# Router logits with the gate as the stationary operand in four column groups, small transfers in front of large ones, and the loop bodies reordered

## The reference, cut to what matters

```python
x = x + xattn(layernorm(x), ctx)      # Q, K, V projections, FFT over the sequence,
                                      # two Hamilton products, a filter, inverse FFT
x = x + ffn(layernorm(x))             # a router and 8 experts
# in ffn:
tokens = layer_norm(inputs.reshape(-1, 512), gamma, beta)
logits = tokens @ gate_weight.T                     # [16384, 8], float32
top1 = argmax(logits);  weight = softmax(logits)[top1]
rank = running count of tokens per expert;  keep = rank < 1024
dispatch[top1, rank] = tokens                       # 8 experts x 1024 slots
h = gelu(dispatch @ wi) ;  expert_out = h @ wo      # 512 -> 2048 -> 512
out = inputs + weight * expert_out[top1, rank]
```

## Time and profile before

| | us |
|---|---|
| median of 3 runs | 3565.24 (3561.56 to 3566.55) |
| profiled execution, its own time | 3560.93 |
| span of the profiled execution | 3559.1 |
| PE busy | 3459.5 (97%) |
| DVE busy | 2547.8 (72%) |
| ACT busy | 1610.9 (45%) |
| POOL busy | 1264.8 (36%) |

### The profile page before, as it was taken

The page is one execution under the profiler, slowest core; times in us unless marked ns, Lnnn a source line. Parts: engine busy times, 40 slices in busy tenths (PEclk is TensorE's granted clock), DMA queues, the critical chain, the costliest instruction groups (busy, mean ns, idle before and its releaser), DMA issues. The chain is left out here.

```text
span 3559.1 us, 46918 instructions
## 1 busy us (share of the span) xinstructions
PE 3459.5 (97%) x15056; PEld 2634.4 (74%) x15056; DVE 2547.8 (72%) x3536; ACT 1610.9 (45%) x2948; POOL 1264.8 (36%) x1607
## 2 busy tenths in 40 slices
PE   7999999999999999999999959999999999999998
PEld 5766777767776777776777648888888888888886
DVE  4999999999999999989899954444444444444443
ACT  4545545455454554545545333333333333333332
POOL 2556656466565565656566530000000000000000
PEclk9999999999999999999999969999999999999999
DMA  5421221211212112121121123333333333333331
GB/s 201 153 104 59 73 83 59 81 62 59 83 48 95 60 59 95 71 83 48 59 95 60 60 81 104 109 119 118 120 119 119 117 119 106 107 105 119 107 108 41
DMA packets 223433, 326.65 MB, mean 92 GB/s; under 512 B 36880, under 2 KB 102672, under 8 KB 223280
## 3 DMA queue, kind: packets, MB, share of 16 engines
q1 hardware_dynamic: 207952, 307.97, 25.1%
q0 software_dynamic: 15360, 16.99, 1.4%
HBM read 256.82 MB, written 101.97 MB: 101 GB/s over the span
## 5 line engine op out<-in xcount | busy, mean ns | idle before, releaser
L1372 ACT ACTIVATE act<-hid_ps 128x512 f32<-128x512 f32 x256 | 153.1, 598 | 797.5 <-PE hid_ps L1299 797.5
L1433 DVE CAST act_h<-act 128x512 fp32r<-128x512 f32 x256 | 109.3, 427 | 523.2 <-ACT act L1372 523.2
L1253 POOL TENSOR_TENSOR tally<-tally,unit 1x1 f32<-1x1 f32 x16 | 2.9, 180 | 1350.2 <-DVE mixed L1445 1350.2
L468 PE MATMUL pair<-w_q,q_spec 128*128 128x512 f32 x1024 | 457.6, 595 | 11.6 <-DVE s L989 10.7
L1299 PE MATMUL hid_ps<-tok_h,w_h 128*128 128x512 f32 x1024 | 405.5, 396 | 0.2 <-issue 0.2
L1299 PE MATMUL hid_ps<-tok_l,w_h 128*128 128x512 f32 x1024 | 399.3, 390 | 0.0
L1299 PE MATMUL hid_ps<-tok_h,w_l 128*128 128x512 f32 x1024 | 398.7, 389 | 0.0
L1315 PE MATMUL out_ps<-w_l,act_h 128*128 128x512 f32 x1024 | 398.5, 389 | 0.0
L1314 PE MATMUL out_ps<-w_h,act_l 128*128 128x512 f32 x1024 | 398.3, 389 | 0.0
L1313 PE MATMUL out_ps<-w_h,act_h 128*128 128x512 f32 x1024 | 398.3, 389 | 0.0
L1427 DVE TENSOR_TENSOR w_l<-w_raw,w_h 128x2048 fp32r<-128x2048 f32 x128 | 293.4, 2293 | 90.9 <-ACT w_h L1366 90.9
(11 more groups left out here) (172 smaller groups left out, 7931.5 us busy)
## 6 DMA issues: line engine op xcount, KB each, us to landing
w_raw<-in_L_ffn_wi SPq DMA_DIRECT2D x128, 512.0 KB, 3.5
w_raw<-in_L_ffn_wo SPq DMA_DIRECT2D x128, 512.0 KB, 4.5
w_raw<-in_x SPq DMA_DIRECT2D x32, 1024.0 KB, 5.4
w_raw<-in_ctx SPq DMA_DIRECT2D x32, 1024.0 KB, 7.7
x_res<-in_x SPq DMA_DIRECT2D x31, 1024.0 KB, 9.8
out<-x_res SPq DMA_DIRECT2D x31, 1024.0 KB, 4.3
slots<-rows SPq DMA_DIRECT2D x4, 4160.0 KB, 17.3
got<-slots SPq DMA_DIRECT2D x15, 1040.0 KB, 7.6
```

Of the source, the lines that this page charges most:

```text
L468: last = nc.tensor.matmul(pair[k % 2][:, s, :], spec[:, c, tile * 256 + s * P:tile * 256 + (s + 1) * P], w[:, c, :], start=(c == 0 and n = ...
L1253: nc.gpsimd.tensor_tensor(tally[:], tally[:], unit[:], ALU.add).then_inc(tallied, 1)
L1372: nc.scalar.activation(act32[i % 2][:], hid_ps[i % 2][:], ACT.Gelu).then_inc(gelu, 1)
L1433: v.tensor_copy(act_h[i % 4][:], act32[i % 2][:]).then_inc(ah_ready, 1)
```

## The change

1. **Logits.** The gate is now the stationary operand, padded with zeros from 8 to 32 columns (`gate_w`), and 256 tokens are streamed at once. The four blocks of 128 features go to four column groups of the array (`tile_position=(0, 32 * c)`) and end as four partial sums on partitions 32c to 32c+31 of `even_ps`, 4 matmuls for each half sequence. When both halves are there, ACT copies `even_ps` to SBUF (`logits_out`, into the first half of `x_tok_t`, called `parts`), and PE adds the four partial sums and turns the result in one product (`logits_turn`): `parts` stationary, 128 x 128, with the 0/1 matrix `chosen` of 8 columns streamed, four of them, into columns 64 to 95 of `odd_ps`. `choose` reads the logits there. The two new semaphores are `logit_ev` and `logit_ready`; one small constant more is loaded.
2. **SP's list.** `real_store` and `real_out` come first, `real_spread` stands before `load_x`, and `real_spread`, `real_gather` belong to sequence b-2 instead of b-3; `load_c` stands before `load_x`.
3. **Bodies.** The bodies of PE, ACT, POOL and DVE are written in a new order, given in full below. On PE the order of a sequence is spread over bodies b to b+4, with `project(k=4)` split over two bodies, and the turns and logits no longer stand together. `choose(b - 3)` stands at the end of DVE's body, `scatter(b - 5)` replaces `scatter(b - 3)` on POOL.

```diff
+            gate_w = sb("gate_w", [P, CB, 32])
+            gate_g = gate_w[:, :, 0:EXPERTS]
+            chosen = sb("chosen", [P, EXPERTS])
...
-            x_tok_t = [sb(f"x_tok_t{i}", [P, CB, P]) for i in (0, 1)]
+            x_tok_t = sb("x_tok_t", [P, 2, CB, P])
+            parts = x_tok_t[:, 0].rearrange("p c e -> p (c e)")
...
                     def body(b):    # SP
-                        real_spread(b - 3)
-                        real_gather(b - 3)
                         real_store(b - 3)
+                        real_out(b - 2)
                         store(b - 4)
-                        real_out(b - 2)
+                        load_c(b)
+                        real_spread(b - 2)
                         load_x(b)
-                        load_c(b)
                         load_res(b - 3)
+                        real_gather(b - 2)
...
                     # inverse(b, 0, 0) now waits for the copy of the logits
-                                pe.wait_ge(route, (b - 1) * ROUTE + 1)
+                                pe.wait_ge(logit_ev, b)
...
-                    def logits(b, t):
-                        pe.wait_ge(g_ev, b * 4 + t + 1)
-                        if t == 0:
+                    def logits(b, h):
+                        pe.wait_ge(g_ev, b * 4 + 2 * h + 2)
+                        if h == 0:
                             pe.wait_ge(unfold, b * UNF + UNF)
                         for c in range(CB):
-                            last = nc.tensor.matmul(even_ps[:, t * EXPERTS:(t + 1) * EXPERTS], x_tok_t[t % 2][:, c, :],
-                                                    gate_g[:, c, :], start=(c == 0), stop=(c == CB - 1))
+                            last = nc.tensor.matmul(even_ps[32 * c:32 * c + 32, h * 256:h * 256 + 256], gate_w[:, c, :],
+                                                    x_tok_t[:, :, c, :], start=True, stop=True, tile_position=(0, 32 * c))
                         last.then_inc(logit_mm, 1)
+                    def logits_turn(b):
+                        pe.wait_ge(logit_ev, b + 1)
+                        for t in range(ROWT):
+                            o = LOGITS + t * EXPERTS
+                            last = nc.tensor.matmul(odd_ps[:, o:o + EXPERTS], parts[:, t * P:(t + 1) * P], chosen[:],
+                                                    start=True, stop=True)
+                        last.then_inc(logit_ready, 1)
...
                     # ACT
                     def token_block(b, t):
                         act.wait_ge(g_mm, b * 4 + t + 1)
-                        wait(act, logit_mm, b * 4 + t - 1)
+                        if t < 2:
+                            wait(act, logit_ready, b)
+                        else:
+                            act.wait_ge(logit_mm, b * 2 + 1)
...
+                    def logits_out(b):
+                        act.wait_ge(logit_mm, b * 2 + 2)
+                        nc.scalar.activation(parts, even_ps[:], ACT.Copy).then_inc(logit_ev, 1)
```

More of the change, by code:

```diff
@@ L544, in body @@
                     def body(b, p):
-                        logits(b - 3, 1)
-                        logits(b - 3, 2)
+                        project(b - 2, 4, 1)
+                        dft(b - 1, 1, 0)
+                        dft(b - 1, 1, 1)
+                        ranks(b - 4)
+                        project(b - 2, 5, 0)
+                        project(b - 2, 5, 1)
+                        inverse(b - 3, 0, 1)
+                        dft(b - 1, 1, 2)
+                        dft(b - 1, 1, 3)
@@ new lines, in body @@
+                        inverse(b - 3, 1, 0)
+                        inverse(b - 3, 1, 1)
+                        turn(b - 3, 1 - p, 0)
+                        project(b - 1, 0, 0)
+                        project(b - 1, 0, 1)
+                        turn(b - 3, 1 - p, 1)
+                        turn(b - 3, 1 - p, 2)
+                        project(b - 1, 1, 0)
+                        project(b - 1, 1, 1)
+                        logits(b - 3, 0)
+                        project(b - 1, 2, 0)
@@ L557, in body @@
+                        inverse(b - 2, 0, 0)
+                        project(b - 1, 3, 1)
+                        project(b - 1, 4, 0)
                         dft(b, 0, 3)
[L558 to L577, removed]
@@ L578, in _ @@
-                    for b in range(6):
+                    for b in range(7):
                         body(b, b % 2)
[L580 to L583, removed]
+                    with pe.Fori(7, 29, 2) as b:
+                        body(b, 1)
+                        body(b + 1, 0)
+                    for b in range(29, BATCH + 4):
                         body(b, b % 2)
@@ L728, in body @@
[L728 to L734, removed]
                         spectrum(b - 1, 1, 0)
                         spectrum(b - 1, 1, 1)
+                        real_part(b - 2, 4)
+                        context_high(b - 1)
                         spectrum(b - 1, 1, 2)
-                        real_part(b - 2, 4)
+                        real_part(b - 2, 5)
@@ L739, in body @@
                         spectrum(b - 1, 1, 3)
+                        sums_x(b)
+                        squares_x(b)
                         token_block(b - 3, 0)
                         sums_x2(b - 3, 1 - p)
[L742 to L745, removed]
                         token_block(b - 3, 1)
                         real_part(b - 1, 0)
-                    for b in range(7):
+                        real_bin(b - 1, 0)
@@ L749, in _ @@
+                        base_of(b - 3, 1 - p)
+                        q_of(b)
+                        real_part(b - 1, 3)
+                        exps(b - 3)
+                        spectrum(b, 0, 2)
+                        spectrum(b, 0, 3)
+                    for b in range(6):
                         body(b, b % 2)
[L750 to L753, removed]
+                    with act.Fori(6, 30, 2) as b:
+                        body(b, 0)
+                        body(b + 1, 1)
@@ L754, in _ @@
+                    for b in range(30, BATCH + 3):
                         body(b, b % 2)
@@ L894, in body @@
                     def body(b, p):
-                        mean2(b - 3)
-                        mean1(b)
[L897 to L903, removed]
+                        stats1(b - 1)
+                        mean2(b - 4)
+                        start1(b - 1)
+                        stats2(b - 4, p)
+                        scales1(b - 1)
+                        scatter(b - 5, 1 - p)
+                        real_bins(b - 2)
+                        mean1(b)
+                    for b in range(8):
                         body(b, b % 2)
-                    with pool.Fori(6, 30, 2) as b:
+                    with pool.Fori(8, 30, 2) as b:
                         body(b, 0)
                         body(b + 1, 1)
-                    for b in range(30, BATCH + 3):
+                    for b in range(30, BATCH + 5):
                         body(b, b % 2)
```

84 lines of the change are left out of this document (45 added, 39 removed).

## The result

The changed kernel takes 3477.58 us (median of 4 runs, 3476.09 to 3477.75) against 3563.4 for the kernel before beside it: a ratio of 0.9759, 95% interval 0.9742 to 0.9776, 86 us faster. The forecast was 3541, range 3498 to 3580. The direction was right, the size was off by more than a factor of three.

What follows compares the result with a forecast made beforehand. PE was taken to bound the first part. Logits -13, array changes +21, waits -15, clock -9, start -3, end -5 gave -24 from 3560.9: 3537, or 3541 on the median's scale; range 3498 to 3580 us.

Steps and rivals of the forecast that it cites:

- Logits on PE: PE's logits calls and logits_turn: 2.97 us a sequence, 0.41 less than before, -13 us in all.
- five steps of 0.216, 1.08 us: One logits call on PE: second pass of each group runs beside the next group's first, no wider.
- rival 1: Logits on PE: all four column groups run at once, -55 us in place of -13, time 3499; chance 0.18.
- My bound for it by weight loads: Logits on PE: loads every 0.1 us, 0.8 us a group, would hold the -55 at about -30, time 3524.
- Rival 2: Logits on PE: the four groups run one after the other, +28 us in place of -13, time 3582; chance 0.16.
- its limit for "slower": Serial logits case: slower from 0.7 us a body more than before, drains included; its own case was 1.54 us.
- Going in and out: PE array: four layout changes a body at 0.16 us each, +21 us (0 to +45).
- Waits and the new order: PE's 17.7 us of waits fall to about 3 with choose at DVE's end: -15 us (-18 to +15).
- The margins I worked out for DVE: DVE's results ready before PE needs them, every margin about 2 us or more.
- The clock: PE's five falls to half clock in the steady part vanish, 1.8 us each: -9 us (-9 to 0).
- SP's order: SP's transfer list: real-bin transfers come one body earlier, load_res directly follows load_x, nobody waits: 0 us.
- Start and end: Start: PE's 3.96 us wait for w_vl, -3 us (-5 to 0); end of first part: -5 us (-12 to +6).

Runs made afterwards that it cites:

- runs 5 and 6: Changed kernel with two column groups instead of four, two feature blocks in each, issued 0,0,1,1 and 0,1,0,1: 3501.72 and 3501.85 us.
- run 1: Changed kernel's new order with the old logits product (turned tokens stationary, 8 gate columns streamed), no logits_turn: 3543.09 us, 0.9932 of the kernel before.
- run 9: Changed kernel with SP's old list: 3475.23 us, 0.9722 of the kernel before.
- runs 1 and 10: Run 10, beside run 1: changed kernel with four transposes for logits_turn and one more DVE reduction adding the partial sums: 3474.29 us.

## Why the prediction was wrong

**Logits on PE: the step that failed.** I put a call at five steps of 0.216, 1.08 us, because "PE starts matmuls in order" and the two passes of a matmul share a group. The second half is true, the first is not: runs 5 and 6 show that each column group works through its own sequence whatever the order of issue. A call takes 0.57. The term was to be -13; the product's calls come to 2 x 0.57 + 0.81 = 1.95 against 3.40, -46 us over 32 sequences. This was rival 1's mechanism, to which I gave 0.18. My bound for it by weight loads was wrong too: a load for one group of 32 columns does take 0.11 us, but the loads of the four groups run beside each other as well, and all eight lie within 0.16 us. (Rival 2 has a slip: the other terms give 1.0 us a body, so its limit for "slower" is 1.0 and not 0.7; its price and time don't use it.)

The Trainium skill's page "TensorE: Matmul & The Clock Gate", section on packing small matmuls, has four row tiles of 512 columns 3.07 times and three column tiles 2.38 times as fast as one after the other. The traces here agree in kind: four column groups take 0.57 us and one takes 1.85, 3.2 times as much. The same section of the Trainium skill says that matmuls start and end strictly in program order; runs 5 and 6 differ from that, for groups of columns at least, and the measurement decides.

**Going in and out.** I took 0.16 us for each change, +21 us. A call takes 0.14 more than its two passes of 0.216, the `dft` in front of it 0.09 more than usual, and the one behind it 0.02 more than behind the old product: 0.25 a call, 16 us in 64 calls, of which 9 stand within the 0.57 already. With a slow start of 0.09 behind `logits_turn`, 3 us, this makes the product worth 46 less some 10 us; run 1 has 1.11 us a body, 35.5. Right in kind, and near in size.

**Waits and the new order: a term that was sized too small.** I forecast -15, with 3 us of waits left. PE waits for nothing, and run 1 has a body 1.1 us shorter than before (62.10 against 63.2 without falls), 31 us over 28 bodies, although has 17.7 in all. The error is in how I read the earlier trace rows. They count the time in which PE has no record under way, and a record runs on after the next one could have started. What a wait costs is seen from one start to the next. In the kernel before, around one body's two waits:

```profile
1470.78 5.34 PE L442 MATMUL xt_ps<-fwd,q_fold 128*128 128x256 f32 x24
1476.38 1.98 PE L502 MATMUL even_ps<-r_spec,inv 128*128 128x512 f32 x4 [0.26 <-DVE rows L1063]
1478.20 1.88 PE L502 MATMUL odd_ps<-r_spec,inv 128*128 128x512 f32 x4
...
1487.58 0.60 PE L516 MATMUL xt_ps<-eye,rows 128*128 128x128 f32 x4
1488.51 7.13 PE L468 MATMUL pair<-w_q,q_spec 128*128 128x512 f32 x16 [0.33 <-DVE s L989]
1495.48 0.95 PE L527 MATMUL even_ps<-gate_g,x_tok_t 128*128 128x8 f32 x8
```

The same pieces as the last three in run 1, without a wait:

```profile
1512.43 0.60 PE L524 MATMUL xt_ps<-eye,rows 128*128 128x128 f32 x4
1512.87 7.03 PE L476 MATMUL pair<-w_q,q_spec 128*128 128x512 f32 x16
1519.74 1.04 PE L524 MATMUL xt_ps<-eye,rows 128*128 128x128 f32 x8
```

The turn takes 0.93 us in place of 0.44, and the projection behind it 6.97 in place of 6.87: this wait of 0.33 cost 0.59. In the same way the `dft` of 24 records takes 5.60 in place of 24 x 0.216 = 5.18, and the four matmuls behind it 1.82 in place of 1.72: the wait of 0.26 cost 0.52. Together 1.1 us for 0.6 us shown, which is all that run 1's body is shorter by. So the 17.7 us of idle time were worth some 31.

The margins I worked out for DVE held, as far as PE never waits for it; their sizes were not measured. Its own wait is in `choose`, 1.7 us a body, and no one waits for it.

**The clock.** The five falls went, as forecast. By the bodies they were worth some 8 us over 28 (63.5 against 63.2 each), against my 9; this is not isolated.

**SP's order.** Nothing, as forecast (run 9).

**Start and end.** Forecast -3 and -5. The wait of 3.96 us for `w_vl` is gone, as forecast; PE's waits up to 200 us are 19.2 us in place of 23.5. The end behind the 29th `choose` is 14.9 us shorter and the first `choose` 3.5 us later, 11.4 in all, of which some 7 us are three more bodies at 2.5 us each. That leaves about 4 where I had 8.

Put together for the first part, 82.1 us: 48.5 by the order (2110.95 to 2062.43 in run 1), 33.6 by the product (to 2028.84). My sum had -32 for the first and +8 for the second. So 42 us of the miss come from the product, nearly all by the groups that run beside each other, and some 16 from the order, most of it by the waits that the earlier trace rows show too short. The order was measured as a whole: which engine's new list brings what was not tried.

## What to carry to other kernels

Where an engine's records overlap, read the cost of its waits from one start to the next and not from its idle time: here 0.6 us of idle time a body stood for 1.1 us. A narrow stationary operand is worth its four column groups, and they need no special order of issue, but each group should get as few passes as possible; count the longest sequence in one group. A faster product that adds a hop to another engine must come with an order that puts other work under the hop: in the one place tried in the old order it cost 105 us, in the new one it brought 36.

## What the runs showed of the hardware that was not expected

- Column groups run side by side even in float32, with two passes each: 0.57, 0.99 and 1.85 us for 2, 4 and 8 passes in the longest group.
- Going from the full array into the column groups cost 0.09 us in front of a call; the call took 0.14 more than its passes, and the slow start behind it, 0.10, was 0.02 more than behind the old product.
- Weight loads of different column groups run beside each other: eight loads of 32 columns, 0.11 us each, lay within 0.16 us.
- The length of a part that nobody touched moved from 1447 to 1479 us with the number of instructions in front of it, by five stalls of 4 us at the loop over experts, and 32 tiny matmuls elsewhere put it back. The loop's program was loaded again in each turn in some versions (39 packets from 2450 to 3250 us) and not at all in others; the stalls came in two of those that load (runs 1 and 10), and in none that does not. A difference of 1% between two versions of a large program can be this and nothing else; the length of the untouched part tells.
- The kernel before took 3563, 3567 and 3565 us beside three sets of runs and 3575 beside the fourth, on another chip, with a clock of 0.980 to 0.983 there. On that same chip the changed kernel with SP's old list took 3475, no more than the changed kernel elsewhere. So the 10 us belong to the kernel before and not to the chip alone; more falls of the clock would fit, and no trace of it there shows them.
